# A gated two-layer transformer block on one core: the second attention written out batch by batch, and its key padding added by products of 32 rows

## The chip, the cores and the metric

The kernel runs on one core of a Trainium2 chip. The metric is the device time of one execution in microseconds (us); lower is better. The core has a matrix engine (PE, whose weight loads are listed as PEld), three others that compute (DVE, ACT, POOL), a queue that issues transfers (SP), and memory that is read over DMA queues. Each engine works through its own instruction stream in order and waits for others by semaphores. PE writes only into eight accumulation banks, and the other engines copy out of them.

## What is computed

Two layers on x (32 batches of 128 rows of 128 numbers), each an attention to a context of 77 keys and then a routed feed-forward, both scaled by gates. The change lies in the second attention:

```python
q, k, v = proj(query, Wq, bq), proj(key, Wk, bk), proj(value, Wv, bv)   # 16 heads of 8
scores = jnp.einsum('bhqd,bhkd->bhqk', q, k) * scale[None, :, None, None]
scores = scores + _rel_bias(bias_table, tq, tk)[None]
neg = -jnp.finfo(scores.dtype).max
scores = jnp.where(key_padding_mask[:, None, None, :], neg, scores)
attn = jax.nn.softmax(scores, axis=-1)
out = jnp.einsum('bhqk,bhkd->bhqd', attn, v)
out = out.transpose(0, 2, 1, 3).reshape(b, tq, DIM)
out = out @ Wo + bo
```

The second feed-forward picks for each row one of eight 128x128 maps by the largest of eight scores. The padding mask is an input, one byte for each batch and key.

## The kernel before, in words

Four stages follow each other: the first attention (`attend_0`, to about 110 us), the first feed-forward (a shared part and 39 sorted tiles of rows, to about 220 us), and then `attend_1`, which holds both the second attention and the second feed-forward and works batch by batch to the end.

In `attend_1` each engine has a list of stages, each with a lag: `pipeline(pe, B, [(signature, 5), (weigh(0), 3), ...])` runs, in every turn, each stage once, for the batch that is `lag` turns behind. The order in the list is the order on the engine. `pipeline` writes the first turns out as straight code (8 batches on PE), runs the middle ones in a hardware loop of two batches (12 passes, whose addresses and semaphore values come from registers), and writes the last turns out again.

PE's stages for one turn, in order from the middle of the list: `queries` (L1244), `probs_T(0)` (L1266, four transposes), `heads_T` (L1290), `picked_bias` (L1327, a product of 8 rows), `scores(0)` (L1253, L1257), `norm3_T` (L1306), `probs_T(1)`, `mixed_T` (L1295), `norm_T` (L1240), `signature` (L1310), `weigh` (L1279, four products of 77 rows, each into 32 columns), `maps(0)` (L1318, a product of 512 columns), `scores(1)` (L1253, L1257), `weigh(3)`, `maps(1)` (L1318).

`scores(half)` makes the scores of eight heads in two banks. In each bank a product of ones with the padding row comes first (L1253: `onesb` is 128x128 ones, `padR` holds the padding in partition 0 and zeros in the others, both bf16), and on top of it come the scores of four heads (L1257: 32 rows of the array, one group of rows for each bank, f32). An f32 product is recorded as two passes, each with its own weight load; a transpose or a bf16 product as one. PE rows are labelled rows*columns: `32*128` are 32 rows of the array.

DVE reads the scores (`bias`, L1446), finds the maxima (L1453), does the softmax shift (`subtract`, L1467), chooses the map (`choose`, L1500 to L1507), multiplies the four chosen maps (`pick`, L1514) and adds the residual (`add_bias`, L1523). `norm3_T` on PE waits for `add_bias` of the batch before; `maps(1)` waits for `pick(0)`.

The padding bytes come to one partition by one transfer (`late[0]`), a memset on POOL zeroes `padR` at the start (L825), and DVE scales them in (L1130).

Of the kernel before, what the change touches and what calls it, by code (L numbers as in the profile page):

```python
# [21 lines left out]
U8 = mybir.dt.uint8  # L22
ALU = mybir.AluOpType
# [3 lines left out]
B, S, D = 32, 128, 128  # L27
FILLS = 12
SPARE = 128 * FILLS
SK = 77  # L30
# [3 lines left out]
HG = 4  # L34
# [21 lines left out]
PADDED = -(2.0 ** 100)  # L56
# [59 lines left out]
def wait(eng, sem, value):  # L116

    if isinstance(value, int) and value <= 0:
        return
    eng.wait_ge(sem, value)  # L120
# [8 lines left out]
def pipeline(eng, n, stages, ways=2, begin=None):  # L129

    first = min(lag for _, lag in stages)
    stages = [(stage, lag - first) for stage, lag in stages]
    span = max(lag for _, lag in stages)
    head = -(-(span + ways) // ways)
    tail = -(-(n + span) // ways)

    def turn(i):
        if begin:  # L140
            begin(i)
        for u in range(ways):
            for stage, lag in stages:
                item = ways * i + u - lag
                if isinstance(item, int) and not 0 <= item < n:
                    continue
                stage(item, (u - lag) % ways)

    for i in range(head):
        turn(i)  # L150
    with eng.Fori(head, n // ways) as i:
        turn(i)
    for i in range(n // ways, tail):
        turn(i)


def written_out(n, stages):
# [30 lines left out]
def build(nc, a, out):  # L188
    with ExitStack() as ctx:
        def sb(name, shape, dt=F32):  # L190
            return ctx.enter_context(nc.sbuf_tensor(name, shape, dt))
# [34 lines left out]
        onesb = sb("onesb", [128, 128], BF16)  # L226
# [11 lines left out]
        rows = sb("rows", [128, WR])  # L238
# [18 lines left out]
        b2 = sb("b2", [T, D])  # L257
        biasQ = sb("biasQ", [128, NH, SK])
        padR = sb("padR", [128, B, SK], BF16)
        padRi = sb("padRi", [1, B * SK], U8)  # L260
        nmax = sb("nmax", [128, B])
        slot = sb("slot", [128, B], U32)
        tile_experts = sb("tile_experts", [1, WORDS], I32)
# [97 lines left out]
def attend_0(nc, sb, sem, sems, bank, a, m, f, units):  # L361
# [54 lines left out]
    spread = lambda t: t.rearrange("p (o d) -> p o d", o=1).to_broadcast([128, PAIR, D])  # L416

    late = [
        (m["padRi"][:, :], a["pad"].rearrange("(o n) -> o n", o=1)),
        (sorted_x[E * REGION:E * REGION + 512], a["spare"][E:E + 4].rearrange("t p d -> (t p) d")),  # L420
        (sorted_x[E * REGION + 512:E * REGION + DUMPS * 128], a["spare"][E:E + DUMPS - 4].rearrange("t p d -> (t p) d")),
        *[(m["wgu"][:, 2 * k:2 * k + 2, :], a["wgu"][:, 2 * k:2 * k + 2, :]) for k in range(E // 2)],
# [394 lines left out]
    def pool_program(pool):  # L817
# [3 lines left out]
        nc.gpsimd.memset(m["quarter"][:, :], D / 4.0).then_inc(s["q"], 1)  # L821
        for u in two:
            nc.gpsimd.memset(V0[u][:, :, D:D + 1], 1.0)
        nc.gpsimd.memset(m["onesb"][:, :], 1.0)
        nc.gpsimd.memset(m["padR"][:, :, :], 0.0)  # L825

        step = [0]

# [55 lines left out]
def feed_forward_0(nc, sb, sem, sems, bank, a, m, units):  # L884
# [6 lines left out]
    pad = sb("pad", [1, E])  # L891
# [176 lines left out]
    def dve_program(dve, clear, n_late):  # L1068
# [58 lines left out]
        add(1)  # L1127
        gated(w2[:, :, :], 3)
        nc.vector.tensor_scalar(b2[:, :], b2[:, :], tg[0:T, 3:4], None, ALU.mult)
        nc.vector.tensor_scalar(m["padR"][0:1, :, :].rearrange("p b k -> p (b k)"), m["padRi"][:, :], PADDED, None, ALU.mult)  # L1130
        clear(dve)
        for c in range(3, NC):
            product(c)
# [27 lines left out]
def attend_1(nc, sb, sem, sems, bank, out, m, f, units):  # L1161

    X, K1T, V1, power, ident = (m[k] for k in ("X", "K1T", "V1", "power", "ident"))
    headmask, biasQ, padR, onesb, routed = (m[k] for k in ("headmask", "biasQ", "padR", "onesb", "routed"))
# [46 lines left out]
    bS, bP, bO, bA, bB, bF = bank[0:2], bank[2:4], bank[4], bank[5], bank[6], bank[7]  # L1211
# [11 lines left out]
    def pe_program(pe):  # L1223
# [22 lines left out]
        def scores(half):  # L1246
            def stage(b, u):
                if half == 0:
                    pe.wait_ge(s["qs"], b + 1)
                    pe.wait_ge(s["kb"], b + 1)  # L1250
                wait(pe, s["sb"], NHF * b + half)
                for i in two:
                    nc.tensor.matmul(bS[i][:, 0:HG * SK], onesb[:, :],  # L1253
                                     padR[:, bass.ds(b, 1), :].to_broadcast([128, HG, SK]), start=True, stop=False)
                for i in two:
                    rows = slice(32 * (2 * half + i), 32 * (2 * half + i) + 32)
                    nc.tensor.matmul(bS[i][:, 0:HG * SK], QT[u][rows, :], KB[u][rows, :, :],  # L1257
                                     start=False, stop=True).then_inc(s["sc"], 1)
            return stage
# [65 lines left out]
        def picked_bias(b, u):  # L1325
            pe.wait_ge(s["pk"], 2 * b + 2)
            nc.tensor.matmul(bF[:, 0:128], OHT[u][:, :], b2[:, :], start=True, stop=True).then_inc(s["fb"], 1)  # L1327

        pipeline(pe, B, [
            (signature, 5), (weigh(0), 3), (probs_T(2), 3), (weigh(1), 3), (probs_T(3), 3), (choice_T, 5),  # L1330
            (project, 4), (weigh(2), 3), (maps(0), 5), (scores(1), 2), (weigh(3), 3), (maps(1), 5),
# [4 lines left out]
    def act_program(act):  # L1336
# [60 lines left out]
        def choice_T(b, u):  # L1397
            act.wait_ge(s["hT"], b + 1)
            wait(act, s["fb"], b - 1)
            nc.scalar.activation(OHT[u][:, :], bF[0:T, 0:128], ACT.Copy).then_inc(s["hTs"], 1)  # L1400

        pipeline(act, B, [
            (shared("pe0"), 0), (probs_T(0), 2), (shared("norm2"), 0), (norm2, 0), (norm3_T, 4),
            (probs_T(1), 2), (mixed_T, 3), (shared("xTs"), 0), (norm_T, 0), (probs_T(2), 2), (choice_T, 4),
# [12 lines left out]
    def dve_program(dve):  # L1417
# [102 lines left out]
        def add_bias(b, u):  # L1520
# [3 lines left out]
                                           in1=x3[u][:, :], op0=ALU.add, op1=ALU.add).then_inc(s["x3b"], 1)  # L1524

        pipeline(dve, B, [
            (choose, 5), (shared("bias0"), 0), (bias(0), 2), (shared("max0"), 0), (maxima(0), 2),
            (lower(0), 2), (residual, 4), (pick(0), 5), (shared("bias2"), 0), (bias(1), 2),
# [124 lines left out]
```

## Time and profile before

| what | value |
| --- | --- |
| median of 3 runs | 575.73 us (575.27 to 578.17) |
| span of the profiled execution, first to last instruction | 572.2 us |
| what lies around the span, taken as median less span | 3.5 us |
| PE busy | 518.1 us, 91% |
| DVE busy | 397.8 us, 70% |
| POOL busy | 366.0 us, 64% |
| ACT busy | 341.6 us, 60% |
| chain that ended last: share of PE | 69% |

The busy shares are averages over stages that differ. The profiled execution's own time outside the profiler is not recorded, so the median of the runs stands for it. In the windows of the trace a PE busy share of 1.00 still holds time in which the array does nothing useful, since a matmul is recorded from the moment its weight load begins to its modelled end; the spacing between starts tells more than the durations.

### The profile page before, as it was taken

The page shows a single profiled execution, that of the slowest core. Times are in us where ns is not written, and L with a number is a line of the kernel's source. Part 1 is how long each engine was busy: PE and PEld are TensorE (multiplying, and loading weights), DVE is VectorE, ACT ScalarE, POOL GpSimd, SP SyncE. Part 2 cuts the span into 40 slices and gives each one's busy share as a digit, 9 for nine tenths or more (in the row PEclk, how much of TensorE's full clock was granted, in tenths as well). Part 3 has the DMA queues.
Part 4 walks back from the last instruction along what each step waited for, and adds up shares of the span by engine and source line. Part 5 has one row for each costly group of instructions (what it writes and reads, how often), then busy time and mean ns, then how long its engine had stood idle before and what let it go on. Part 6 is the DMA issues. An engine that isn't in the chain of part 4 may idle for free.

```text
span 572.2 us, 14118 instructions
## 1 busy us (share of the span) xinstructions
PE 518.1 (91%) x3611; PEld 335.8 (59%) x3611; DVE 397.8 (70%) x1174; ACT 341.6 (60%) x997; POOL 366.0 (64%) x781
## 2 busy tenths in 40 slices
PE   6878886699999996899999999999999999999952
PEld 5767775456566655565656565665656565656520
DVE  3868887375334433578888888888888888888631
ACT  3667775322455552787676767677676767676510
POOL 4665888774255554346777777777777786777442
PEclk9978997599999999999999999999999999999965
DMA  9934620131122221000000000000000000000000
GB/s 229 154 72 132 174 60 16 37 85 46 43 75 79 76 62 38 10 6 15 11 13 18 9 18 9 18 9 18 9 18 9 18 9 18 9 9 5 10 10 5
DMA packets 32280, 23.79 MB, mean 42 GB/s; under 512 B 7897, under 2 KB 29793, under 8 KB 32210
## 3 DMA queue, kind: packets, MB, share of 16 engines
q1 hardware_dynamic: 29250, 17.86, 12.8%
q0 software_dynamic: 2272, 4.67, 2.5%
q10 hardware_dynamic: 720, 0.82, 0.6%
q8 instruction: 16, 0.26, 0.2%
q14 instruction: 22, 0.18, 0.1%
HBM read 16.57 MB, written 8.39 MB: 44 GB/s over the span
## 4 chain that ended last, share of the span: by engine, by line
PE 69%; POOL 5%; DVE 3%; DMA 3%; issue 3%; ACT 3%; POOLq 0%; SPq 0%; DVEq 0%; ACTq 0%
PE bank L1318 12%; PE bank L1266 11%; PE bank L1279 8%; PE bank L1257 8%; PE bank L1002 4%; PE bank L1253 3%; PE bank L1290 2%; PE bank L1327 2%; PE bank L1018 2%; DMA xs<-sorted_x 2%; PE bank L956 2%; PE bank L957 2%; PE bank L967 2%; PE bank L1306 1%; PE bank L1244 1%
## 5 line engine op out<-in xcount | busy, mean ns | idle before, releaser
L1367 ACT ACTIVATE PRT<-bank 77x512 f32<-77x512 f32 x128 | 74.7, 584 | 17.7 <-PE bank L1266 15.7
L1266 PE MATMUL bank<-cst,wgu 128*77 128x128 f32 x512 | 81.0, 281 | 1.0 <-ACT wgu L1359 1.0
L1318 PE MATMUL bank<-w,xn3T 128*128 128x512 f32 x128 | 75.0, 668 | 2.5 <-DVE XN L1514 2.0
L1266 PEld LDWEIGHTS bank<-cst,wgu 128*77 128x77 f32 x512 | 59.5, 150 | 15.5 <-issue 13.9
L1359 ACT ACTIVATE wgu<-wgu,low 128x77 f32<-128x77 f32 x256 | 67.4, 346 | 1.3 <-DVE low L1460 0.2
L946 POOL DMA_INDIRECT routed<-ys,to x39 | 37.4, 959 | 45.0 <-DVE ys L1149 34.1
L1446 DVE TENSOR_TENSOR wgu<-bank,biasQ 128x616 f32<-128x616 f32 x64 | 51.1, 799 | 11.5 <-PE bank L1257 9.9
L1514 DVE TENSOR_TENSOR XN<-bank,OH 128x512 f32<-128x512 f32 x64 | 44.3, 692 | 16.3 <-PE bank L1318 10.8
L1279 PE MATMUL bank<-PRT,VP 77*32 77x128 f32 x1024 | 54.5, 285 | 0.5 <-ACT PRT L1367 0.5
L1453 DVE TENSOR_REDUCE top<-wgu 128x8 f32<-128x616 f32 x64 | 50.5, 789 | 1.1
L1257 PE MATMUL bank<-KB,QT 32*128 32x308 f32 x256 | 50.7, 472 | 0.0
L1581 POOL TENSOR_TENSOR wgu<-XN 128x512 f32<-128x512 f32 x32 | 40.5, 1265 | 15.1 <-DVE XN L1514 15.1
L1144 DVE TENSOR_TENSOR hid<-actg,bank 128x256 f32<-128x256 f32 x39 | 16.4, 421 | 40.5 <-ACT actg L1053 40.5
L1002 PE MATMUL bank<-wgu,xsT 128*128 x78 | 40.7, 604 | 0.4 <-ACT xsT L1048 0.4
L1560 POOL TENSOR_TENSOR x2b<-x,rows 128x128 f32<-128x128 f32 x32 | 14.5, 455 | 39.8 <-DVE x L1488 39.8
L814 POOL DMA_INDIRECT sorted_x<-XN,slot x32 | 34.0, 1062 | 8.5 <-issue 8.2
L1583 POOL TENSOR_TENSOR wgu<-wgu 128x256 f32<-128x256 f32 x32 | 35.7, 1116 | 2.5
L1279 PEld LDWEIGHTS bank<-PRT,VP 77*32 77x32 f32 x1024 | 20.2, 108 | 24.3 <-issue 18.3
L1467 DVE TENSOR_TENSOR wgu<-wgu,top 128x616 f32<-128x616 f32 x32 | 33.3, 1040 | 0.0
L1395 ACT ACTIVATE xn3T<-bank 128x128 f32<-128x128 f32 x32 | 8.9, 278 | 36.7 <-PE bank L1306 36.7
L1318 PEld LDWEIGHTS bank<-w,xn3T 128*128 128x128 f32 x128 | 19.6, 193 | 17.4 <-ACT OHT L1400 6.9
L1257 PEld LDWEIGHTS bank<-KB,QT 32*128 32x128 f32 x256 | 19.3, 184 | 17.0 <-issue 17.0
(231 smaller groups left out, 1268.1 us busy)
## 6 DMA issues: line engine op xcount, KB each, us to landing
xs<-sorted_x SPq DMA_DIRECT2D x39, 64.5 KB, 1.8
wgu<-in_wgu SPq DMA_DIRECT2D x4, 512.0 KB
y<-routed SPq DMA_DIRECT2D x32, 64.0 KB, 1.8
out<-res SPq DMA_DIRECT2D x32, 64.0 KB, 1.6
ctxT<-in_ctxT SPq DMA_DIRECT2D x16, 77.0 KB, 2.9
mask<-in_mask SPq DMA_DIRECT2D x16, 77.0 KB, 3.4
wdn<-in_wdn SPq DMA_DIRECT2D x2, 512.0 KB
X<-in_x SPq DMA_DIRECT2D x1, 768.0 KB, 5.7
```

The lines of the kernel that those rows point to most:

```text
L946: nc.gpsimd.indirect_dma_start(routed, bass.IndirectOffsetOnAxis(ap=to[:, t:t + 1], axis=0), ys[t % WAYS][:, :], None).then_inc(st_y[t % W ...
L1002: nc.tensor.matmul(bH[t % 2][:, :], xsT[t % 2][:, :], wgu[:, bass.ds(experts[t], 1), :], start=True, stop=True).then_inc(e["h"], 1)
L1257: nc.tensor.matmul(bS[i][:, 0:HG * SK], QT[u][rows, :], KB[u][rows, :, :], start=False, stop=True).then_inc(s["sc"], 1)
L1266: last = nc.tensor.transpose(bP[c % 2][0:SK, j * 128:j * 128 + 128], SC[u][:, c * HG + j, :], ident)
L1279: last = nc.tensor.matmul(bO[32 * j:32 * j + 32, c * 128:c * 128 + 128], VP[u][:, c * HG + j, :], PT[c % 2][:, j * 128:j * 128 + 128], sta ...
L1318: nc.tensor.matmul(bF[:, :], xn3T[u][:, :], w2[:, k * HT:(k + 1) * HT, :], start=True, stop=True).then_inc(s["f"], 1)
L1359: last = nc.scalar.activation(SC[u][:, head, :], SC[u][:, head, :], ACT.Exp, bias=low[u][:, head:head + 1])
L1367: nc.scalar.activation(PT[c % 2][:, :], bP[c % 2][0:SK, :], ACT.Copy if c * HG < HH else ACT.Exp).then_inc(s["pTs"], 1)
L1446: nc.vector.tensor_tensor(half(SC[u][:, k, :]), bSS, half(biasQ[:, k, :]), ALU.add).then_inc(s["sb"], 1)
L1453: nc.vector.tensor_reduce(top[u][:, k], SC[u][:, k, :], AX.X, ALU.max).then_inc(s["mx"], 1)
L1514: nc.vector.tensor_tensor(picked[u][:, k * HT:(k + 1) * HT, :], bF[:, :].rearrange("p (t d) -> p t d", t=HT), OH[u][:, k * HT:(k + 1) * HT ...
L1581: nc.gpsimd.tensor_tensor(sum4[u][:, :, :], picked[u][:, 0:4, :], picked[u][:, 4:8, :], ALU.add).then_inc(s["s4"], 1)
```

## The change

`pipeline` no longer makes a loop: every turn of every engine's part of `attend_1` is written out. The padding is replicated over all 128 partitions by the transfer; the ones become 1/32; each padding product now takes only the 32 rows (of `onesb` and of `padR`) that the scores of the same bank take. The memset of `padR` on POOL goes, and DVE scales 128 partitions in place of one.

```diff
--- before.py
+++ after.py
@@ -133,25 +133,16 @@
     first = min(lag for _, lag in stages)
     stages = [(stage, lag - first) for stage, lag in stages]
     span = max(lag for _, lag in stages)
-    head = -(-(span + ways) // ways)
-    tail = -(-(n + span) // ways)
-
-    def turn(i):
+    turns = -(-(n + span) // ways)
+
+    for i in range(turns):
         if begin:
             begin(i)
         for u in range(ways):
             for stage, lag in stages:
                 item = ways * i + u - lag
-                if isinstance(item, int) and not 0 <= item < n:
-                    continue
-                stage(item, (u - lag) % ways)
-
-    for i in range(head):
-        turn(i)
-    with eng.Fori(head, n // ways) as i:
-        turn(i)
-    for i in range(n // ways, tail):
-        turn(i)
+                if 0 <= item < n:
+                    stage(item, (u - lag) % ways)
 
 
 def written_out(n, stages):
@@ -257,7 +248,7 @@
         b2 = sb("b2", [T, D])
         biasQ = sb("biasQ", [128, NH, SK])
         padR = sb("padR", [128, B, SK], BF16)
-        padRi = sb("padRi", [1, B * SK], U8)
+        padRi = sb("padRi", [128, B * SK], U8)
         nmax = sb("nmax", [128, B])
         slot = sb("slot", [128, B], U32)
         tile_experts = sb("tile_experts", [1, WORDS], I32)
@@ -416,7 +407,7 @@
     spread = lambda t: t.rearrange("p (o d) -> p o d", o=1).to_broadcast([128, PAIR, D])
 
     late = [
-        (m["padRi"][:, :], a["pad"].rearrange("(o n) -> o n", o=1)),
+        (m["padRi"][:, :], a["pad"].rearrange("(o n) -> o n", o=1).to_broadcast([128, B * SK])),
         (sorted_x[E * REGION:E * REGION + 512], a["spare"][E:E + 4].rearrange("t p d -> (t p) d")),
         (sorted_x[E * REGION + 512:E * REGION + DUMPS * 128], a["spare"][E:E + DUMPS - 4].rearrange("t p d -> (t p) d")),
         *[(m["wgu"][:, 2 * k:2 * k + 2, :], a["wgu"][:, 2 * k:2 * k + 2, :]) for k in range(E // 2)],
@@ -821,8 +812,7 @@
         nc.gpsimd.memset(m["quarter"][:, :], D / 4.0).then_inc(s["q"], 1)
         for u in two:
             nc.gpsimd.memset(V0[u][:, :, D:D + 1], 1.0)
-        nc.gpsimd.memset(m["onesb"][:, :], 1.0)
-        nc.gpsimd.memset(m["padR"][:, :, :], 0.0)
+        nc.gpsimd.memset(m["onesb"][:, :], 1.0 / 32)
 
         step = [0]
 
@@ -1127,7 +1117,7 @@
         add(1)
         gated(w2[:, :, :], 3)
         nc.vector.tensor_scalar(b2[:, :], b2[:, :], tg[0:T, 3:4], None, ALU.mult)
-        nc.vector.tensor_scalar(m["padR"][0:1, :, :].rearrange("p b k -> p (b k)"), m["padRi"][:, :], PADDED, None, ALU.mult)
+        nc.vector.tensor_scalar(m["padR"][:, :, :].rearrange("p b k -> p (b k)"), m["padRi"][:, :], PADDED, None, ALU.mult)
         clear(dve)
         for c in range(3, NC):
             product(c)
@@ -1250,8 +1240,9 @@
                     pe.wait_ge(s["kb"], b + 1)
                 wait(pe, s["sb"], NHF * b + half)
                 for i in two:
-                    nc.tensor.matmul(bS[i][:, 0:HG * SK], onesb[:, :],
-                                     padR[:, bass.ds(b, 1), :].to_broadcast([128, HG, SK]), start=True, stop=False)
+                    rows = slice(32 * (2 * half + i), 32 * (2 * half + i) + 32)
+                    nc.tensor.matmul(bS[i][:, 0:HG * SK], onesb[rows, :],
+                                     padR[rows, b:b + 1, :].to_broadcast([32, HG, SK]), start=True, stop=False)
                 for i in two:
                     rows = slice(32 * (2 * half + i), 32 * (2 * half + i) + 32)
                     nc.tensor.matmul(bS[i][:, 0:HG * SK], QT[u][rows, :], KB[u][rows, :, :],
```

On PE, around `scores(0)` in the loop, before (names of tiles without buffer numbers; `ISA` and `REGISTER_ALU` are the rows that compute addresses and semaphore values, and `[waits ...]` are the semaphores of a row):

```order
L1290 MATMUL bank<-cst,OS 128x128 x3
L1326 REGISTER_ALU
L1327 MATMUL bank<-b,OHT 128x128 [waits d_pk]
L120 REGISTER_ALU [waits d_kb,d_qs]
L1253 ISA [waits d_sb]
L1253 MATMUL bank<-padR,onesb 128x308 x2
L1257 MATMUL bank<-KB,QT 128x308 x2
L1306 MATMUL bank<-cst,xn 128x128 [waits d_x3b,d_xn3]
```

The same place in a written-out turn of the change, whose lines are numbered 9 lower:

```order
L1281 MATMUL bank<-cst,OS 128x128 x3
L1318 MATMUL bank<-b,OHT 128x128 [waits d_pk]
L1244 MATMUL bank<-padR,onesb 128x308 [waits d_sb,d_kb,d_qs]
L1244 MATMUL bank<-padR,onesb 128x308
L1248 MATMUL bank<-KB,QT 128x308 x2
L1297 MATMUL bank<-cst,xn 128x128 [waits d_x3b,d_xn3]
```

No product moved; the register rows are gone and their waits sit on the products. That a padding product takes 32 rows and not 128 can't be seen here, since a row shows what is written.

On DVE, the choice of the map and the first half's bias, in the loop before:

```order
L1500 TENSOR_REDUCE am<-bank 128x1 [waits d_hT,d_sg]
L1501 ISA
L1502 SCALAR_TENSOR_TENSOR am<-bank,am,cst 128x8 [waits d_am]
L1504 REGISTER_ALU
L1505 TENSOR_REDUCE am<-am 128x1 [waits d_am]
L1506 REGISTER_ALU
L1507 TENSOR_SCALAR OH<-am 128x8 [waits d_am]
L1441 ISA
L1446 TENSOR_TENSOR wgu<-bank,biasQ 128x616 [waits d_pT,d_sc]
```

And in the change:

```order
L1493 SCALAR_TENSOR_TENSOR am<-bank,am,cst 128x8 [waits d_am]
L1496 TENSOR_REDUCE am<-am 128x1 [waits d_am]
L1498 TENSOR_SCALAR OH<-am 128x8 [waits d_am]
L1437 TENSOR_TENSOR wgu<-bank,biasQ 128x616 [waits d_pT,d_sc]
```

Here too the work keeps its order and only the register rows go. Over the whole program PE has 1891 such rows in place of 1169, DVE 1144 in place of 735.

## Rows read from the trace of the kernel before

**Rows 1.** Busy time by stretch: engines' us and counts, clock, DMA share, GB/s.

```profile
280.00:320.00 40.00, 40.00 (x330) 24.06 (x323) 34.26 (x82) 28.35 (x82) 29.50 (x66) 1.00 0.05 15
```

**Rows 2.** Chain that ended last: start us, us, what.

```profile
252.28 0.35 ACT wgu L1359
...
252.68 0.66 PE bank L1266 x4
...
253.82 0.27 PE bank L1253 x2
...
526.35 0.37 PE bank L1253 x2
...
532.09 0.27 PE bank L1253 x2
...
534.56 0.57 issue
```

**Rows 3.** Timeline of PE around `scores(0)`, narrow windows: start us, us, engine, line.

```profile
272.60 0.48 PE L1327 MATMUL bank<-b,OHT 8*128 8x128 f32 x2
...
272.81 0.27 PE L1327 MATMUL bank<-b,OHT 8*128 8x128 f32 x1
...
273.01 0.31 PE L1253 MATMUL bank<-padR,onesb 128*128 128x308 bf16 x1
...
273.15 0.30 PE L1253 MATMUL bank<-padR,onesb 128*128 128x308 bf16 x1
...
273.38 0.53 PE L1257 MATMUL bank<-KB,QT 32*128 32x308 f32 x2
...
273.74 0.42 PE L1257 MATMUL bank<-KB,QT 32*128 32x308 f32 x2
...
274.10 0.33 PE L1306 MATMUL bank<-cst,xn 128*128 128x128 f32 x1
...
282.32 0.37 PE L1327 MATMUL bank<-b,OHT 8*128 8x128 f32 x1
```

**Rows 4.** Timeline of PE's weight loads, the same place.

```profile
273.49 0.19 PEld L1257 LDWEIGHTS bank<-KB,QT 32*128 32x128 f32 x2
```

**Rows 5.** Timeline of PE around `scores(1)`.

```profile
277.78 1.12 PE L1318 MATMUL bank<-w,xn3T 128*128 128x512 f32 x2
278.74 0.43 PE L1253 MATMUL bank<-padR,onesb 128*128 128x308 bf16 x2
279.10 0.79 PE L1257 MATMUL bank<-KB,QT 32*128 32x308 f32 x4
279.82 0.43 PE L1279 MATMUL bank<-PRT,VP 77*32 77x128 f32 x8
```

**Rows 6.** Timeline of PE in the first attention: a bf16 product between f32 ones.

```profile
15.84 0.23 PE L503 MATMUL bank<-mb,identb 128*128 128x154 bf16 x1
15.91 0.38 PE L520 MATMUL bank<-cst,P 128*77 128x128 f32 x2
```

**Rows 7.** Timeline of DVE in one period, its waits in brackets.

```profile
273.87 1.06 DVE L1467 TENSOR_TENSOR wgu<-wgu,top 128x616 f32<-128x616 f32 x1
275.30 0.17 DVE L1500 TENSOR_REDUCE am<-bank 128x1 f32<-128x8 f32 x1 [0.37 <-PE bank L1310]
...
279.96 0.80 DVE L1446 TENSOR_TENSOR wgu<-bank,biasQ 128x616 f32<-128x616 f32 x1 [0.33 <-PE bank L1257]
```

**Rows 8.** Timeline of PE and DVE where no scores follow `picked_bias` any more.

```profile
535.29 0.48 PE L1327 MATMUL bank<-b,OHT 8*128 8x128 f32 x2
536.32 0.30 PE L1306 MATMUL bank<-cst,xn 128*128 128x128 f32 x1 [0.55 <-DVE x3b L1523]
```

**Rows 9.** DMA queues that carry instructions: packets, MB, share of 16 engines.

```profile
q8 instruction: 16, 0.26, 0.2%
q14 instruction: 22, 0.18, 0.1%
```

**Rows 10.** The memset of padR: count, least, median, most ns, first and last start.

```profile
L825 POOL MEMSET padR<- x1: 2162/2162/2162, 1.1 to 1.1; 128x2464 bf16 x1
```

## The prediction, made before the changed kernel ran

> **What bounds the kernel now.** The first view to read is the chain of work that ended last. From 252.68 us it stands on PE without a break, stage after stage, until 534.56, where an "issue" row and then DVE take over [rows 2]. So in this stretch of 281.9 us nothing but PE decides. [...] One turn takes 9.73 us: `picked_bias` starts at 272.60 and again at 282.32 in straight code, and the padding of `scores(0)` is at 253.82 and, 28 turns later, at 526.35, which is 9.73 a turn through the loop too [rows 2, 3]. That already says that the loop itself costs nothing now.
>
> The third view is the timeline of PE, read by its starts. A product of 512 f32 columns takes 0.96 us for two passes [rows 5]; with a weight load of 0.10 in front that leaves 0.43 a pass, so 308 columns of f32 take 0.26 a pass, and bf16 takes half, 0.13 (154 columns bf16 are 0.07 in [rows 6], and two padding products start 0.14 apart in [rows 3]). Now `scores(0)`: the last pass of `picked_bias` (8 rows of the array, 128 columns, 0.11) starts at 272.81, but the padding, 128 rows, only at 273.01: 0.09 more than the pass. The second padding product starts at 273.15 and streams to 273.28, but the scores, 32 rows, start at 273.38: again 0.10 more. After the scores' second pass (273.74, two products side by side, 0.26) comes `norm3_T` with 128 rows at 274.10: 0.10 more once again [rows 3]. Where the number of rows does not change, there is no such gap: the bf16 product at 15.84 is followed by an f32 transpose at 15.91, its 0.07 and nothing else, so it isn't the change of type either [rows 6]. I read the 0.09 to 0.10 as the price of changing between 128 and 32 rows (8 rows counting as 32). `scores(0)` pays three of them. `scores(1)` follows `maps(0)`, 128 rows, with no gap, and pays two: before the scores and behind them [rows 5].
>
> The scores also show what two products in different row groups do: both first passes start within 273.38, both second ones within 273.74 [rows 3], side by side. Between them lie 0.36 us, of which 0.26 is streaming: the first weight load, 0.10, lies open, since nothing ran that it could hide under. The second load of each group, at 273.49, lies wholly beside the first pass in the same rows [rows 3, 4].
>
> **The change, part by part.** Padding products of 32 rows, in the row group of their scores. (a) They run side by side and not one behind the other: 0.14 becomes about 0.01, a gain of 0.13 for each half. (b) The scores' first weight load, 0.10, now lies beside a padding product of the same mode that streams for 0.13: gain 0.10 for each half. (c) In `scores(0)` both changes of mode ahead of the scores go, since 8, 32 and 32 rows follow each other: gain 0.09 + 0.10, and the 0.01 of the padding's own load. In `scores(1)` the change between padding and scores only moves ahead of the padding: nothing. So `scores(0)` would run: padding at 272.92, scores at 273.05, second pass 273.31, end 273.57, `norm3_T` at 273.66 in place of 274.10, gain 0.44. `scores(1)`: `maps(0)` ends at 278.74, 0.10 for the mode, padding 278.84, scores 278.98, second pass 279.24, end 279.50, next product 279.59 in place of 279.82, gain 0.23. Together 0.67 us a turn: a period of 9.06.
>
> How often: `scores(0)` stands on the unbroken chain from 253.82 to 526.35, 29 times, and `scores(1)` 29 times up to 532.09 [rows 2]: 29 x 0.67 = 19.4 us. The first turns are partly on ACT's chain (its rows stand just ahead of 252.68 [rows 2]); of the three earlier turns I count between nothing and 3 x 0.44 = 1.3, take 0.5.
>
> Who could take it back: DVE. In the same period it waits 0.37 us for `signature` (L1310) and 0.33 for the scores (L1257), and hardly elsewhere [rows 7]. So DVE could keep a period of 9.73 - 0.70 = 9.03 if its waits all vanished; small waits that the bracket does not name make it somewhat less. PE wants 9.06. The two nearly meet. The link by which it would be felt is `norm3_T`, which waits for `add_bias`: where no scores stand between, `norm3_T` starts 1.03 us behind `picked_bias` and had waited 0.55 for DVE [rows 8]; with the new scores PE gets there 273.66 - 272.60 = 1.06 behind. That is 0.03 of margin. I take 0.04 us lost a turn, 1.2 in all, with bounds of 0 and 0.3 a turn.
>
> Writing out. In the loop, register rows go; none lies in PE's chain now, since the period is 9.73 in straight code as in the loop: 0. What comes is code to be fetched. The instruction queues moved 38 packets in all, with 0.2% and 0.1% of sixteen engines' 572 us [rows 9]: q8's 16 packets took about 1.1 us each. The straight turns before the loop run at the same 9.73 with such packets among them, so fetches are hidden by PE's work; cost 0, and 1.1 us for each that isn't. The memset of 2.16 us on POOL at 1.1 us [rows 10] goes; the first work that POOL has then waits for x, so 0 (bounds: 0 and a gain of 0.5). The padding's transfer, in the first attention, grows by a factor of 128 to 315 KB (128 x 2464 bytes); the view of waits names no wait for a transfer around it, and DVE reads the data only in the next stage: 0, at most a loss of 1. The DVE row that scales it has as many elements in a partition as before: 0.
>
> Sum: 19.4 + 0.5 - 1.2 = 18.7. The span goes from 572.2 to 553.5; with the 3.5 around it, 557.0 against the median of 575.7, which is 3.2% less.
>
> [...] The trace has a second weight load at 273.49 beside a first pass in the same rows, and the second pass starts 0.36 behind the first, so only one load was open [rows 3, 4]. [...]
>
> **Rivals.** R1, the load of the scores stays open behind the padding (or a bf16 padding product isn't followed by a hidden f32 load of 32 rows, which no row shows): gain (b) falls away, 58 x 0.10 = 5.8 us, so 562.8. Against it: [rows 4] and the 0.07 of [rows 6]. [...]
> R2, DVE becomes the bound: if its rows, slowed by meetings with POOL (L1467 took 1.06 us in [rows 7]), hold the period at 9.25 to 9.4, the gain is 29 x 0.33 to 0.48, 10 to 14 us: 562 to 566. For it: the margin of 0.03 and DVE's 0.70 of waits in all. Against it: DVE's longest stretches have the same neighbours as before.
> R3, the products don't become cheaper as said: the array changes mode also between 8 and 32 rows, or the two padding products don't run side by side. Each takes 0.09 or 0.26 from the 0.67; both, 10 us: 567. The pair of scores at 273.38 speaks against the second.
> R4, slower: code fetches. In the loop nothing is fetched; written out, PE and DVE have 722 and 409 more rows, and by the rows per packet of before (1169 for q8's 16 and about as many for the rest) that is 10 to 30 more packets. If each stopped PE for its 1.1 us, that takes 11 to 33 us. It decides from 18 stops on; with 30 the time is 575.7 - 19.9 + 33 = 589. Against it: the straight turns ahead of the loop.
>
> **How the numbers follow.** Forecast, period 9.03 to 9.15: 0.60 (555 to 560). R1 0.10, R2 0.17, R3 0.07, R4 0.06, of which half ends slower and a third within the bound of 0.5% (2.9 us) that a measurement of this kernel can tell from no change. So faster 0.95, same 0.02, slower 0.03. The range takes the forecast, R1 and most of R2: 554.5 to 565.
>
> **What would show it.** Right: the spacing from `picked_bias`' last pass to the padding falls from 0.20 to 0.11 or less, from padding to scores from 0.23 to 0.13, the two padding products start together, the turns of `picked_bias` are 9.06 to 9.10 apart, and PE still stands on the chain. R1: padding to scores 0.23 with one load open. R2: turns of 9.2 or more, a wait of `norm3_T` or `maps(1)` for DVE in brackets, the waits of L1500 and L1446 gone. R4: gaps on PE of about 1 us with no engine to wait for. The sum goes wrong above all if a wait that now lies under 0.03 to 0.1 us of margin comes to the front.

## The result, and the profile after

The change runs in 554.9 us (median of 4 runs, 549.3 to 558.4) beside 577.0 us for the kernel before on the same chip: a ratio of 0.9593, 95% interval 0.9544 to 0.9642. Against the 575.7 us shown ahead of the prediction that is 552.3 us, 4.1% less, where 557.0 (3.2% less) was forecast with a range down to 554.5. The direction and the mechanism of the padding were right; the size was too small, and the time lies 2.2 us below the range. The run of 558.4 us counted as slow and is not in the ratio. The interval of the ratio is wide, 549.5 to 555.1 us. The profiled span is 553.2 us in place of 572.2.

The timeline of PE answers to [rows 3] and [rows 5]. This is one turn of the changed kernel, around `scores(0)`, `scores(1)` and the next `picked_bias`:

```profile
372.68 0.37 PE L1318 MATMUL bank<-b,OHT 8*128 8x128 f32 x1
372.69 0.30 PE L1244 MATMUL bank<-padR,onesb 32*128 32x308 bf16 x1
372.89 0.27 PE L1318 MATMUL bank<-b,OHT 8*128 8x128 f32 x1
372.90 0.52 PE L1248 MATMUL bank<-KB,QT 32*128 32x308 f32 x1
373.00 0.29 PE L1244 MATMUL bank<-padR,onesb 32*128 32x308 bf16 x1
373.14 0.68 PE L1248 MATMUL bank<-KB,QT 32*128 32x308 f32 x3
373.75 0.33 PE L1297 MATMUL bank<-cst,xn 128*128 128x128 f32 x1
...
377.37 1.12 PE L1309 MATMUL bank<-w,xn3T 128*128 128x512 f32 x2
378.43 0.30 PE L1244 MATMUL bank<-padR,onesb 32*128 32x308 bf16 x2
378.57 0.68 PE L1248 MATMUL bank<-KB,QT 32*128 32x308 f32 x4
379.18 0.42 PE L1270 MATMUL bank<-PRT,VP 77*32 77x128 f32 x8
...
381.68 0.37 PE L1318 MATMUL bank<-b,OHT 8*128 8x128 f32 x1
```

Read the starts. From the last pass of `picked_bias` (372.89) the bank that ends last has its padding at 0.11, its scores at 0.25, and `norm3_T` follows at 0.86; before, it was 0.20, 0.57 and 1.29 [rows 3]. In `scores(1)`, `maps(0)` to padding is 1.06, padding to scores 0.14, scores to the next product 0.61: 1.81 in all against 2.04 [rows 5]. The turn is 9.01 us (9.735 before), and PE still decides. Busy time by stretch, columns as in [rows 1], has it at 40.00 of 40.00 us, with DVE nearer to it than before (36.13 in place of 34.26 [rows 1]):

```profile
280.00:320.00 40.00, 40.00 (x353) 25.22 (x352) 36.13 (x90) 30.35 (x88) 32.05 (x74) 1.00 0.06 18
```

The weight loads show how the load of the scores is hidden. In `scores(1)` they start with the padding products, and the scores stand 0.14 behind these:

```profile
378.42 0.09 PEld L1244 LDWEIGHTS bank<-padR,onesb 32*128 32x128 bf16 x2 [0.76 <-issue]
378.43 0.33 PEld L1248 LDWEIGHTS bank<-KB,QT 32*128 32x128 f32 x4
```

The chain that ended last, cut to where it changes engine, answers to [rows 2]. PE carries it alone from 254.78 to 508.34; then DVE has pieces of it in the last turns:

```profile
254.78 0.66 PE bank L1257 x4
...
508.34 0.04 DVE x3b L1514
...
509.10 1.25 DVE wgu L1458
```

The two instruction queues moved 68 packets in place of 38 [rows 9]. Of the 68, 38 lie between 256 and 509 us, and no turn there is longer than 9.02 us, so these fetches cost nothing there:

```profile
q8 instruction: 31, 0.51, 0.4%
q14 instruction: 37, 0.30, 0.2%
```

Where the 19.0 us of span came from is read off two rows, `norm3_T` of all 32 batches (count, least, median and most ns, first and last start). Before:

```profile
L1306 PE MATMUL bank<-cst,xn x32: 299/328/445, 254.7 to 553.8; 128*128 128x128 f32 x32
```

After:

```profile
L1297 PE MATMUL bank<-cst,xn x32: 299/328/447, 256.6 to 535.1; 128*128 128x128 f32 x32
```

Between first and last, 299.1 became 278.5: 20.6 us gained in the turns. Behind the last, 18.4 became 18.1. Ahead of the first, 254.7 became 256.6: 1.9 us lost. The forecast had 18.7 for the whole span and so looks right. That is luck: the turns gave more than was forecast, and the later start hides it. The experiments take the two apart.

### The profile page after: what moved, and what is told of

Its sections match the earlier page's. It is cut to its first block, busy times and chain, and to the rows that moved or that the text cites. A ratio compares the mean times of both kernels' runs of the same rounds, so it can differ in the third digit from the quotient of the medians.

```text
span 553.2 us, 12766 instructions
## 1 busy us (share of the span) xinstructions
PE 500.8 (91%) x3611; PEld 332.6 (60%) x3611; DVE 394.0 (71%) x1174; ACT 340.7 (62%) x997; POOL 361.3 (65%) x780
## 4 chain that ended last, share of the span: by engine, by line
PE 70%; POOL 5%; DVE 3%; DMA 3%; issue 3%; ACT 1%; POOLq 0%; SPq 0%; DVEq 0%
PE bank L1309 13%; PE bank L1257 12%; PE bank L1270 8%; PE bank L1248 7%; PE bank L992 5%; PE bank L1008 2%; PE bank L1281 2%; PE bank L1318 2%; PE bank L946 2%; PE bank L947 2%; PE bank L957 2%; DMA xs<-sorted_x 2%; PE bank L1244 2%; PE bank L1297 1%; PE bank L1234 1%
## 5 line engine op out<-in xcount | busy, mean ns | idle before, releaser
L1257 PE MATMUL bank<-cst,wgu 128*77 128x128 f32 x512 | 81.0, 281 | 0.6 <-ACT wgu L1350 0.6
L1257 PEld LDWEIGHTS bank<-cst,wgu 128*77 128x77 f32 x512 | 58.4, 148 | 14.9 <-issue 7.9
L1244 PE MATMUL bank<-padR,onesb 32*128 32x308 bf16 x128 | 28.0, 306 | 0.0
L1043 ACT ACTIVATE actg<-bank 128x256 f32<-128x256 f32 x39 | 15.0, 385 | 20.1 <-PE bank L992 20.1
```

The source lines that it names most:

```text
L1244: nc.tensor.matmul(bS[i][:, 0:HG * SK], onesb[rows, :], padR[rows, b:b + 1, :].to_broadcast([32, HG, SK]), start=True, stop=False)
L1257: last = nc.tensor.transpose(bP[c % 2][0:SK, j * 128:j * 128 + 128], SC[u][:, c * HG + j, :], ident)
```

## The experiments

"Turn" is the median distance of `norm3_T` over twenty turns in the middle; ratios are to the kernel before on the same chip, with their 95% interval. Single executions of one kernel differ by several us, so steps below half a per cent are read from the turn.

| run | turn, us | ratio |
| --- | --- | --- |
| kernel before, run again (e0) | 9.735 | 1.0015 (0.9987 to 1.0043) |
| before, ACT alone written out (e8) | 9.68 | 0.9986 (0.9957 to 1.0015) |
| before, all written out (e1) | 9.68 | 0.9936 (0.9903 to 0.9970) |
| padding of 64 rows (e6) | 9.78 | 1.0033 (0.9993 to 1.0072) |
| change, only PE written out (e2) | 9.13 | 0.9725 (0.9693 to 0.9757) |
| change, DVE in its loop (e5) | 9.11 | 0.9645 (0.9586 to 0.9704) |
| change, ACT in its loop (e3) | 9.07 | 0.9663 (0.9634 to 0.9692) |
| the change, run again (e4) | 9.01 | 0.9595 (0.9548 to 0.9641) |
| change, transfer last (e10) | 9.01 | 0.9648 (0.9612 to 0.9685) |
| change, padding doubled (e9) | 9.28 | 0.9796 (0.9767 to 0.9825) |
| change, `picked_bias` in rows 96 to 103 (e11) | 8.95 | 0.9633 (0.9601 to 0.9665) |
| change, no padding (e7) | 8.91 | 0.9560 (0.9502 to 0.9619) |

**e0, the kernel before again.**

> The kernel before, unchanged, as a control. Every theory expects a ratio of 1.00 within 0.5%, a turn of 9.73 us, and stages ahead of the second attention that vary by some us from execution to execution with the granted clock (the second attention's first padding product was at 229.8 us before and at 231.4 us after the change). It also shows what lies around the span in the same execution: 2.0 us was measured after the change, 3.5 us was assumed before it.

Measured: turn 9.735, 573.49 us for the profiled execution and 571.3 for its span. So 2.2 us lie around the span (2.2 to 2.35 in each of the 12 executions), and not the 3.5 that the prediction took as median less span. The other 1.3 of the 3.5 is that the execution profiled there was shorter than the median.

**e1, writing out alone.** The diff's part on `pipeline` without the rest; the padding stays at 128 rows.

> Only the writing out, on all engines; the padding products stay at 128 rows, from padR with the padding in partition 0. Theory A (ACT's register row in front of norm3_T's copy is in PE's chain): signature starts 0.71 us behind norm3_T's product in every turn, not 0.78, so the turn falls from 9.73 to 9.67 and the time by 26 x 0.063 = 1.6 us, ratio 0.997. Theory B (the loop costs nothing, as predicted, and the 0.06 came from the padding products): 9.73, ratio 1.00. Theory C (code fetches stop PE now and then): more than 9.73 in single turns.

Measured: turn 9.68, 0.06 less than before. The ratio excludes 1; what was expected, 0.997, lies at the edge of its interval. Behind the last `norm3_T` it has the 18.1 us of the change in place of 18.4.

**e2, the padding of 32 rows with PE alone written out.** ACT, DVE, POOL and SP keep their loops (`flat` is the change's `pipeline`, `pipeline` here that of before):

```diff
-        pipeline(pe, B, [
+        flat(pe, B, [
```

> The padding products of 32 rows with PE written out; ACT, DVE, POOL and SP keep their loop of two batches. [...] Theory A: signature again 0.78 behind norm3_T, and DVE's add_bias starts about 0.1 later behind picked_bias, which with 0.06 of margin holds norm3_T back by 0.04: a turn of 9.01 + 0.06 + 0.04 = 9.11, 2.6 us more than the change. Theory B: a turn of 9.01, the time of the change.

Measured: turn 9.13, alternating between 9.10 and 9.16; this part alone gives some 0.61 of the 0.725. 9.11 was expected. `norm3_T` stands 0.91 behind the last pass of `picked_bias`, as in e5 below, in place of 0.86, and the signature's load 0.75 behind `norm3_T`, between the change's 0.71 and the 0.78 that was expected. What makes the turns alternate is open.

**e3, ACT back in its loop.** The change, with only ACT looped (`looped` is the `pipeline` of before):

```diff
-        pipeline(act, B, [
+        looped(act, B, [
```

> The changed kernel, but ACT alone keeps its loop of two batches. Theory A: signature 0.78 behind norm3_T in the turns in which ACT is in its loop and 0.71 in the others; turns of 9.07, 26 x 0.063 = 1.6 us more than the change. Theory B: a turn of 9.01 and the same time as the change.

Measured: turn 9.07, as expected. The link that the expectation names is that from `norm3_T` through ACT's copy to the load of the signature. Here:

```profile
374.36 0.33 PE L1325 MATMUL bank<-cst,xn 128*128 128x128 f32 x1
374.81 0.28 ACT L1414 ACTIVATE xn3T<-bank 128x128 f32<-128x128 f32 x1 [0.57 <-PE bank L1325]
...
375.13 0.30 PEld L1329 LDWEIGHTS bank<-wc,xn3T 128*128 128x128 f32 x2
```

And in the change, whose `norm3_T` starts at 373.75:

```profile
374.11 0.28 ACT L1386 ACTIVATE xn3T<-bank 128x128 f32<-128x128 f32 x1 [0.49 <-PE bank L1297]
...
374.46 0.30 PEld L1301 LDWEIGHTS bank<-wc,xn3T 128*128 128x128 f32 x2
```

And in the kernel before:

```profile
371.59 0.33 PE L1306 MATMUL bank<-cst,xn 128*128 128x128 f32 x1
372.04 0.28 ACT L1395 ACTIVATE xn3T<-bank 128x128 f32<-128x128 f32 x1 [1.01 <-PE bank L1306]
372.37 0.30 PEld L1310 LDWEIGHTS bank<-wc,xn3T 128*128 128x128 f32 x2
```

The copy starts 0.45 behind the product in both kernels with ACT in its loop, and 0.36 in straight code; the signature's load 0.77 and 0.78 against 0.71.

**e4, the change again.**

> The changed kernel, unchanged, timed again beside the following three on one chip. Theory A (0.67 us a turn from the padding products, 0.063 from ACT's register row, no turn bound by DVE): 29 x 0.67 + 26 x 0.063 = 21 us less than before from the turns, less about 1 to 2 us that the stretches ahead of the steady turns lost in the profiles with 32 rows so far: a ratio of 0.965 to 0.967. If the 0.959 of the first measurement stands, something of 3 us outside the turns is still unnamed.

Measured: 554.35 us, turn 9.01. The turn was as expected; the ratio, 0.9595, was not: 0.965 to 0.967 was expected, and the interval ends at 0.9641. So the 3 us outside the turns that the expectation calls unnamed stay so (the two medians by themselves, 554.35 and 575.63, give 0.963). The profiled execution has a span of 555.5 at the same turn, 2.3 more than the first: 1.1 of it lies ahead of the first `norm3_T` (257.7 in place of 256.6) and 1.0 in the last turn (10.0 in place of 9.0). That is how far single executions lie apart.

**e5, DVE back in its loop.** As e3, for `pipeline(dve, B, [`.

> The changed kernel, but DVE alone keeps its loop of two batches. Theory A: add_bias starts 0.414 and not 0.308 us behind picked_bias; norm3_T on PE, with a margin of some 0.06 to 0.08 on that chain, comes 0.03 late, PE's next transposes 0.02 behind that, and subtract after the branch costs 0.06 every other turn: a turn of 9.06 to 9.10, 1.5 to 2.5 us more than the change. Rival: DVE has room, a turn of 9.01.

The link from `picked_bias` through `add_bias` to `norm3_T` in the timeline:

```profile
373.50 0.27 PE L1346 MATMUL bank<-b,OHT 8*128 8x128 f32 x1
373.91 0.35 DVE L1542 SCALAR_TENSOR_TENSOR x3b<-bank,dead,x 128x128 f32<-128x128 f32 x1 [0.22 <-PE bank L1346]
...
374.41 0.30 PE L1325 MATMUL bank<-cst,xn 128*128 128x128 f32 x1
...
376.29 0.47 DVE L1526 TENSOR_SCALAR OH<-am 128x8 f32<-128x8 f32 x1
```

Measured: 9.11, above what was expected. `add_bias` starts 0.41 behind `picked_bias` in place of 0.31 (372.89 to DVE's 373.20 in the change), and `norm3_T` stands 0.91 behind the last pass in place of 0.86. That is 0.05 in each turn. Every second turn is another 0.11 longer (9.06 and 9.17), and in each of the longer ones the last row of `choose` (L1526) takes 0.47 to 0.50 us, as above, in place of 0.23 in the turns between; the `pick(0)` behind it starts some 0.26 later, and `maps(1)`, which waits for `pick(0)`, 0.11 later. Why that row takes longer in every second turn of the loop is not shown.

**e6, padding products of 64 rows**, one half of the array for both banks of a half:

```diff
-                    rows = slice(32 * (2 * half + i), 32 * (2 * half + i) + 32)
+                    rows = slice(64 * half, 64 * half + 64)
```

> The changed kernel with padding products of 64 rows (ones of 1/64, rows 0 to 63 for the first half of the heads, 64 to 127 for the second), so that two of them lie in the same rows. Theory M (every change between 128, 64 and 32 rows costs 0.09 to 0.10 us, and products in the same rows run one behind the other): the whole 0.67 is lost again and scores(1) pays a third change, a turn of 9.68 + 0.09 = 9.77, slower than before. Rival M2 (only a change from or to 128 rows costs): picked_bias, padding and scores follow without a gap, a turn of 9.48.

PE's timeline around both halves:

```profile
381.26 1.13 PE L1309 MATMUL bank<-w,xn3T 128*128 128x512 f32 x2
382.32 0.43 PE L1244 MATMUL bank<-padR,onesb 64*128 64x308 bf16 x2
382.69 0.79 PE L1248 MATMUL bank<-KB,QT 32*128 32x308 f32 x4
...
385.91 0.48 PE L1318 MATMUL bank<-b,OHT 8*128 8x128 f32 x2
386.32 0.43 PE L1244 MATMUL bank<-padR,onesb 64*128 64x308 bf16 x2
386.69 0.79 PE L1248 MATMUL bank<-KB,QT 32*128 32x308 f32 x4
```

Measured: turn 9.78, 0.10 above e1. Padding of fewer rows buys nothing here. Padding to scores is 0.37, as with 128 rows; and `maps(0)` to padding is 1.06 in place of 0.96 [rows 5], so 128 to 64 rows costs one more change of mode, of 0.10. Of the three sizes measured, only the one whose rows are those of the scores gains.

**e7, no padding.** The change without the two padding products of each half, so this kernel leaves the key padding out.

> The changed kernel without the padding products (the part of the computation that adds the key padding is left out; the scores start their banks themselves). Theory A (PE is the bound, DVE stands close behind): PE alone would fall by 2 x 0.137 to 8.74, but norm3_T would wait for add_bias and DVE, whose own work fills 8.9 us, takes over: a turn of 8.87 to 8.95, 1.7 to 4 us less than the change. Rival (DVE has the room): 8.74, 8 us less.

The same places of PE's timeline:

```profile
379.81 0.27 PE L1314 MATMUL bank<-b,OHT 8*128 8x128 f32 x1
379.92 0.68 PE L1244 MATMUL bank<-KB,QT 32*128 32x308 f32 x3
380.61 0.30 PE L1293 MATMUL bank<-cst,xn 128*128 128x128 f32 x1
...
384.23 1.13 PE L1305 MATMUL bank<-w,xn3T 128*128 128x512 f32 x2
385.28 0.79 PE L1244 MATMUL bank<-KB,QT 32*128 32x308 f32 x4
386.00 0.42 PE L1266 MATMUL bank<-PRT,VP 77*32 77x128 f32 x8
```

Measured: turn 8.91, only 0.10 less than the change, as expected. In `scores(1)` the padding's 0.13 goes, but the scores then take 0.72 and not 0.61: their first weight load has lost its cover. So 0.04 is left (1.77 against 1.81). Term (b) seen from the other side: the padding in the rows of its scores costs next to nothing. In `scores(0)`, `norm3_T` stands 0.80 behind the last pass in place of 0.86, the place at which e11 (below) has it waiting for `add_bias`.

**e8, ACT alone written out**, in the kernel before: the edit of e2 on `pipeline(act, B, [`.

> The kernel before with ACT's part of the second attention alone written out; PE, DVE, POOL and SP keep their loops, and the padding stays a product of 128 rows. Theory: in the steady turns of the kernel before, the only thing that the loop costs is ACT's late copy of norm3_T, because ACT's loop reads the wait from a register. Then writing out ACT alone gives the whole of what writing out every engine gave: from the product of norm3_T to the first weight load of the signature 0.713 us in place of 0.776, the turn 9.68 us in place of 9.735, the span 1.5 to 2 us shorter, a ratio near 0.997. Rival: the gain needs PE's own stream written out (its waits and addresses come from registers too). Then the turn stays at 9.73 and the ratio at 1.000.

Measured: the copy at 0.36 behind the product, turn 9.68, the same as e1. So in the kernel before the loop cost its 0.06 a turn through ACT alone. The rival, that PE's own stream must be straight, is out. The time can't tell it: the interval of 0.9986 covers both 1.000 and the 0.997 of the theory.

**e9, each padding product twice**, with ones of 1/64:

```diff
-                for i in two:
-                    rows = slice(32 * (2 * half + i), 32 * (2 * half + i) + 32)
+                for k in two:
+                    for i in two:
...
+                                         padR[rows, b:b + 1, :].to_broadcast([32, HG, SK]), start=(k == 0), stop=False)
```

> The change with every padding product made twice: ones of 1/64 in place of 1/32, and two products of 32 rows for each bank, so eight in a turn in place of four. Theory: the padding lies on the path of PE in each turn, and a pair of products of 308 columns in two row groups costs 0.13 us, as one product of 308 columns alone; four more products make two more pairs, so the turn is 9.27 us in place of 9.01, and the time about 7.7 us more than the change. Rival: in scores(0) the extra product of the second bank hides beside picked_bias, as the first one does, and only the other bank's counts; since both banks must end, the pair's time is still set by the bank of rows 0 to 31, so this gives 9.27 too, but if all of the padding of scores(0) hid there it would be 9.14. Rival: DVE has little slack and the later scores hold it up, which adds more than 0.26, 9.35 or above.

PE's timeline at `scores(0)`, the last two padding products of the bank that ends last:

```profile
381.43 0.30 PE L1245 MATMUL bank<-padR,onesb 32*128 32x308 bf16 x1
...
381.57 0.29 PE L1245 MATMUL bank<-padR,onesb 32*128 32x308 bf16 x1
381.71 0.67 PE L1249 MATMUL bank<-KB,QT 32*128 32x308 f32 x3
```

Measured: turn 9.28, 0.27 more: 0.13 to 0.14 for each pair, as term (a) had it; the second pair has no load left to hide, so it costs its full 0.13. The ratio is 0.015 above that of e10, which has the change's turn and ran beside it on the same chip (8.5 us; 29 x 0.27 is 7.8).

**e10, the padding's transfer last** in `late` in place of first:

```diff
     late = [
-        (m["padRi"][:, :], a["pad"].rearrange("(o n) -> o n", o=1).to_broadcast([128, B * SK])),
```

> The change with the padding's transfer to 128 partitions moved from the head of the list of late transfers to its end. Theory: the transfer (2464 bytes to each of 128 partitions in place of 2464 bytes in all) costs nothing that can be seen, and the 1 to 2 us by which the steady turns begin later than in the kernel before come from the granted clock at the start of the second attention. Then the turn is 9.01 and the first norm3_T starts as late as in the change, 255 to 258 us, the ratio to the kernel before 0.957 to 0.963. Rival: the transfer holds up the ones behind it; then the first norm3_T starts 1 us or more earlier than in the change with the same clock ahead of it, and the ratio falls to 0.957 or less.

Here `norm3_T` first starts at 253.0 and not 256.6, as the rival said, but the clock ahead of it is not the same. Busy time by stretch (the last columns are granted clock, DMA share, GB/s) of the change:

```profile
228.00:232.00 4.00, 3.00 (x15) 2.56 (x17) 1.15 (x4) 2.27 (x6) 3.08 (x10) 0.72 0.06 16
232.00:236.00 4.00, 4.00 (x15) 1.98 (x11) 2.08 (x4) 1.07 (x3) 0.87 (x3) 0.50 0.06 18
```

And of e9, which has the transfer first, as the change has:

```profile
228.00:232.00 4.00, 4.00 (x29) 2.56 (x28) 2.72 (x6) 2.09 (x5) 2.52 (x7) 1.00 0.08 22
232.00:236.00 4.00, 3.11 (x25) 2.26 (x23) 1.77 (x5) 3.97 (x11) 2.80 (x8) 1.00 0.04 10
```

e9 has the full clock there, as e10 has, and starts its first `norm3_T` at 252.3, earlier than e10; e11 (below), also with the transfer first, at 252.8. The kernel before shows the same on its own: first `norm3_T` at 254.7 with a granted clock of 0.62 from 228 to 232 us, at 253.1 in e0 with 1.00. So the late start of the change goes with a stretch of a lower granted clock, 0.72 from 228 to 232 us and 0.50 from there to 240, and for the kernel before, whether and where it falls differs between two executions. Both profiled executions of the change have it (e4, with 0.54 and then 0.50, starts at 257.7); whether the change makes it more likely is open. The rival also wanted a ratio of 0.957 or less: the transfer's place shows no gain, and the ratio, 0.9648, is if anything above the change's.

**e11, `picked_bias` in rows 96 to 103**, so that the padding of both banks can lie beside it:

```diff
-            nc.tensor.matmul(bF[:, 0:128], OHT[u][:, :], b2[:, :], start=True, stop=True).then_inc(s["fb"], 1)
+            nc.tensor.matmul(bF[:, 0:128], OHT[u][96:96 + T, :], b2[96:96 + T, :], start=True, stop=True).then_inc(s["fb"], 1)
```

> The change with the picked bias' operands (b2 and the one-hot rows) in partitions 96 to 103 in place of 0 to 7, so that the product picked_bias lies in a row group that neither bank of scores(0) takes. Theory: the padding product of rows 32 to 63 already runs beside picked_bias and the one of rows 0 to 31 has to wait for it to leave its rows; now both run beside it and scores(0) starts earlier. PE by itself would save 0.13 to 0.3 us a turn, but norm3_T waits for add_bias, 0.775 us behind the last pass of picked_bias, and it stands at 0.851 now, so no more than 0.08 comes off there, and DVE's own turn is 8.91: a turn of 8.92 to 8.94 us and 2 to 3 us less than the change. Rival 1: moving the small product to another row group costs a gap of its own and nothing is gained, 9.01. Rival 2: norm3_T isn't held, because picked_bias itself moves ahead, and the turn falls to 8.75 to 8.85.

PE's timeline at `scores(0)`:

```profile
386.41 0.37 PE L1318 MATMUL bank<-b,OHT 8*128 8x128 f32 x1
386.42 0.30 PE L1244 MATMUL bank<-padR,onesb 32*128 32x308 bf16 x2
386.56 0.42 PE L1248 MATMUL bank<-KB,QT 32*128 32x308 f32 x2
386.62 0.27 PE L1318 MATMUL bank<-b,OHT 8*128 8x128 f32 x1
...
387.43 0.30 PE L1297 MATMUL bank<-cst,xn 128*128 128x128 f32 x1 [0.19 <-DVE x3b L1514]
```

Measured: both padding products start with `picked_bias`, and the scores run beside its second pass. PE is 0.26 us earlier, and gets 0.06 of it: `norm3_T` now waits 0.19 for `add_bias`, 0.81 behind the last pass of `picked_bias`. A third of the turns are at 9.0 or more; their cause is open. The time (555.5 beside e10's 555.2) shows no gain where 2 to 3 us were expected, so no version measured here that still adds the padding beats the change.

## Why the prediction was off, point by point

**(a), (b), (c), the three parts of 0.67 a turn: right, to 0.01.** `scores(0)` was to save 0.44 and `scores(1)` 0.23; the rows after show 0.43 and 0.23, and the padding's starts stand where the forecast had them. e6 shows that it is the shared group of rows that pays, e9 that a pair costs the 0.13 of one. R1, the open load, is out: the scores stand 0.14 behind their padding, not 0.23. Only the last `scores(1)`, behind 509 us, gave less: that turn went from 8.95 to 8.86, 0.10 in place of 0.23, and there the chain has DVE in it.

**The hidden load of (b) is in the trace.** In `scores(1)` the scores' loads at 378.43 lie beside the padding of the same rows, which starts at 378.43, and both banks' scores start 0.14 behind it, at 378.57.

**"Writing out: 0" is the step that failed.** It argued from a turn of 9.73 in straight code and in the loop alike. At 272.60, where the straight turn was read [rows 3], PE is still in straight code, but ACT is already in its loop: its straight head is shorter. The two turns compared were both turns with ACT looped. The first two turns of the kernel before, with ACT straight, are 9.68, and would have shown it. Price: 0.06 in each of the 26 turns in which ACT was looped, 1.6 us. e1, e3 and e8 show it from both sides, and that in the kernel before it is ACT alone. That it is the wait carried by a register row is argued from the order of instructions (the loop has such a row ahead of the copy) and not tested by itself. Another 0.3 us went behind the last `norm3_T`: 18.4 in e2, where ACT, DVE, POOL and SP loop, and 18.1 in e1, e3 and e5, so it was the price of POOL's loop or of SP's. And in one and the same execution the time around the span is 2.2 us before (e0) and 2.0 in the change (555.17 less 553.2), 0.2 less. That makes 2.1 us in place of 0.

**The DVE loss of 1.2 us didn't come.** The margin on the link from `picked_bias` through `add_bias` to `norm3_T` was put at 0.03 us, from [rows 8]. Measured, `norm3_T` can stand 0.80 to 0.81 behind the last pass (e7, e11) and stands at 0.86: 0.05. [rows 8] is a written-out turn, so its margin was fit for the changed kernel, and the 0.04 a turn that I took on top of it, for small waits, was caution with no row behind it. It would have been right in kind, and too small, for a kernel with DVE in a loop: there the loss is 0.10 a turn (e5). R2 is the next bound all the same: at 8.91 to 8.95 the turn stops following PE (e7, e11).

**The early turns gave nothing.** The forecast had 0.5 us for them and 0.44 for the one `scores(0)` ahead of the first `norm3_T`. That `norm3_T` started 1.9 us later in the profiled execution, and in e10, with the full clock ahead of it, at 253.0 as in e0.

**The time around the span** was taken as 3.5 us, a median less the span of another execution, where e0 has 2.2. That did no harm by itself, since the same 3.5 stood on both sides of the difference.

**What the sum is now.** From the traces: 20.3 us in the turns (28 turns up to 509 us and the 0.10 of the next), 0.3 behind them, 0.2 around the span, nothing ahead of them: 20.8 us, so 554.9 from 575.7. That is the median measured, 554.9, but the kernel before had a median of 577.0 beside it. The ratio of 0.9593 stands for 23.4 us, with an interval of 20.6 to 26.3. So the traces reach only the near end of the interval, and no run here names the remaining 2.6 us; e10, with the same turn, has a ratio that stands for 20.3. In the profiled execution, writing out (1.6 and 0.3) and the DVE loss that didn't come (1.2) are 3.1 us more than forecast; the late start (1.9), the 0.94 of the early turns and 0.13 in the last `scores(1)` take it back. That is why its span agreed with the forecast, 553.2 and 553.5.

**R3** is out by the rows of `scores(0)`: no gap between 8 and 32 rows beyond 0.11, and the pairs side by side. **R4**, the fetches: 30 more packets came, the upper end of what was estimated, and none is seen in the steady turns. In the kernel before, six of the 38 lie between 256 and 300 us, two between 300 and 340, and none from there to 515. **Memset and transfer**: no cost seen (e10); under about 1 us the spread of the early stages hides it.

**The range** ended at 554.5. That lower end had DVE's link at its cheap end, but it took "writing out" as exactly 0; with the 2.1 us found it would have ended at 552.4, next to the 552.3 of the ratio. It also had no room for the spread of the measurement itself, 549.3 to 558.4 us for single executions of the change.

## What to carry to other kernels

Where an accumulating product only adds a small term, try it in the very rows of the array that its partners take. Here the two padding products of `scores(1)` then started together (378.43), the load of the scores was hidden (padding to scores 0.14 us in place of 0.36), and `scores(0)` was spared its two changes of mode ahead of the scores, of 0.09 and 0.10: 0.67 us off a turn of 9.68 (e1, and 9.01 in e4). And before "straight code and loop run alike" is used as evidence, look up for each engine on the chain, not for PE alone, which turns are straight. Ask the same of each margin: in which form of code was it read?

## What the runs showed of the hardware

- In the hardware loops of these kernels, work behind another engine started later than in straight code: ACT's copy 0.45 us behind PE in place of 0.36, DVE's `add_bias` 0.41 in place of 0.31 (e3, e8, e5).
- Products whose rows were free overtook others. At 372.69 the padding of rows 32 to 63 starts ahead of the second pass of `picked_bias` (372.89), which was issued before it, and the first scores of that bank (372.90) ahead of the other bank's padding (373.00). So PE's stream, which is said above to be worked through in order, was not followed strictly between passes in different rows of the array. A row of the trace tells how many rows of the array a product takes and not which; that the early one is the bank of rows 32 to 63 is read from e11, where `picked_bias` is in rows 96 to 103 and both padding products start beside it.
- A change from 128 to 64 rows costs the same 0.10 us as one from 128 to 32: `maps(0)` to padding is 1.06 in e6 and in the change, and 0.96 with padding of 128 rows.
- Two executions of the kernel before differ by 1.7 us ahead of their first `norm3_T` (254.7 and 253.1), with a granted clock of 0.62 and of 1.00 between 228 and 232 us.
- The profile of the kernel before has two passes for each f32 product of the second attention: 128 products of scores are listed as L1257 x256, the 32 of `picked_bias` as L1327 x64. It has one pass for each transpose (`norm3_T` L1306 x32, `probs_T` L1266 x512, both f32) and one for each bf16 product (the 128 padding products, L1253 x128). Weight loads are as many as passes: 3611 of PEld and 3611 of PE, L1257 x256 in both. The label follows the rows that a product takes: 32 rows are `32*128`, the 64 of the padding in e6 `64*128`.
- A matmul's record started with its weight load where the load lay open: both at 273.38 for the scores before. It did not where the load was hidden: the load of the first padding product of `scores(1)` is at 278.31, its product at 278.74.
- `subtract` (L1467) on DVE took 0.79 us with no POOL instruction beside it (at 238.98) and 1.06 with L1581 and L1583 of POOL beside it (at 273.87). But it took 0.79 at 536.58 too, with L1583 beside it for 0.73 us, so not every meeting slowed it.
